# Cross-attention scores from float32r halves: four products stacked along the contraction, with loop orders and PSUM banks laid out anew

## The reference, cut to what matters

```
x  = layernorm(x + linear_attention(x))         # causal, relu features, out_w
q  = x; k = v = ctx                             # 16 heads of 8
scores = einsum('bhqd,bhkd->bhqk', qh, kh) / sqrt(8)
scores = where(|q - k| > 64, -inf, scores)
x  = layernorm(x + softmax(scores) @ v @ W_proj.T + b_proj)
x  = layernorm(x + switch_ffn(x))               # 8 experts, top 1, capacity 641, gelu, width 512
```

## Time and profile before

| | |
|---|---|
| time, median of 3 runs (lowest, highest) | 424.26 us (423.18, 426.59) |
| span of the profiled execution | 423.4 us |
| PE busy, share of the span | 393.0 us, 93% |
| DVE busy | 330.9 us, 78% |
| ACT busy | 269.4 us, 64% |
| POOL busy | 253.0 us, 60% |

### The profile page before, as it was taken

How to read it: one execution, slowest core, us unless ns; L and a number is a source line. 1 busy time by engine, 2 the same in 40 slices (tenths; PEclk the granted TensorE clock), 3 DMA queues, 4 the chain that set the end, 5 groups by cost and what they waited for, 6 DMA issues and landing times.

```text
span 423.4 us, 19225 instructions
## 1 busy us (share of the span) xinstructions
PE 393.0 (93%) x7095; PEld 297.0 (70%) x7095; DVE 330.9 (78%) x1640; ACT 269.4 (64%) x610; POOL 253.0 (60%) x372
## 2 busy tenths in 40 slices
PE   7889999999999999999999999999878999999960
PEld 6556777677777777677777777766566788888750
DVE  5465778889889888898989988878975588877760
ACT  4437777777877777777778776876646344444441
POOL 5243455676675776765775766576653077766653
PEclk8999999999999999999999999999999999999995
DMA  4900000101111011111102123000021334342000
GB/s 112 319 19 15 23 23 15 29 29 28 56 27 30 28 29 41 42 29 28 29 29 53 31 53 96 15 23 10 28 67 36 98 118 138 117 130 89 26 21 21
DMA packets 25859, 22.74 MB, mean 54 GB/s; under 512 B 3623, under 2 KB 21090, under 8 KB 25766
## 3 DMA queue, kind: packets, MB, share of 16 engines
q1 hardware_dynamic: 23430, 17.30, 14.0%
q0 software_dynamic: 2336, 4.20, 3.1%
HBM read 12.46 MB, written 9.58 MB: 52 GB/s over the span
## 4 chain that ended last, share of the span: by engine, by line
PE 74%; ACT 9%; issue 5%; POOL 4%; DVE 3%; DMA 3%; SPq 1%; POOLq 0%; DVEq 0%; ACTq 0%
PE banks L769 13%; PE banks L719 13%; PE banks L1200 8%; PE banks L711 8%; ACT arena L1481 7%; PE banks L731 7%; PE banks L704 6%; PE banks L781 3%; PE banks L848 2%; PE banks L1180 2%; PE banks L797 2%; PE banks L749 2%; PE banks L751 2%; PE banks L750 2%; POOL expert_in L501 1%
## 5 line engine op out<-in xcount | busy, mean ns | idle before, releaser
L1681 DVE TENSOR_REDUCE mx<-banks 128x8 f32<-128x1024 f32 x64 | 77.0, 1220 | 19.5 <-PE banks L719 19.5
L1228 ACT ACTIVATE arena<-banks 128x1024 f32<-128x1024 f32 x64 | 62.1, 1022 | 42.8 <-PE banks L719 42.8
L769 PEld LDWEIGHTS banks<-arena,V 128*32 128x32 f32 x2048 | 53.3, 109 | 30.0 <-ACT arena L1258 23.5
L769 PE MATMUL banks<-arena,V 128*32 128x128 f32 x2048 | 67.5, 275 | 0.6 <-ACT arena L1258 0.3
L1258 ACT ACTIVATE arena<-banks 128x1024 f32<-128x1024 f32 x64 | 62.1, 1022 | 5.8 <-PE banks L711 5.8
L1481 ACT ACTIVATE arena<-banks,b1T 128x321 f32<-128x321 f32 x64 | 33.8, 529 | 42.9 <-PE banks L1180 42.2
L637 POOL DMA_INDIRECT out_x<-ot,idx x40 | 40.3, 1008 | 23.4 <-DVE ot L2314 11.0
L468 POOL TENSOR_TENSOR rs<-ve,minus_half 128x1 f32<-128x1 f32 x32 | 18.2, 569 | 54.5 <-DVE ve L1649 54.5
L485 POOL TENSOR_TENSOR rs<-ve,minus_half 128x2 f32<-128x2 f32 x32 | 23.2, 726 | 38.7 <-DVE ve L1669 38.6
L501 POOL DMA_INDIRECT expert_in<-x,sidx x32 | 35.1, 1098 | 15.1 <-issue 5.3
L462 POOL TENSOR_TENSOR QE<-qT,head_mask 128x512 f32<-128x512 f32 x32 | 33.1, 1034 | 9.4 <-DVE qT L1592 9.3
(11 more groups left out here) (210 smaller groups left out, 974.7 us busy)
## 6 DMA issues: line engine op xcount, KB each, us to landing
w_sb<-in_L_ffn_W SPq DMA_DIRECT2D x16, 256.0 KB, 3.1
EB<-expert_in SPq DMA_DIRECT2D x9, 325.0 KB, 4.0
expert_in<-zeros SPq DMA_DIRECT2D x10, 266.5 KB, 3.3
X<-in_x SPq DMA_DIRECT2D x32, 64.0 KB, 2.0
C<-in_ctx SPq DMA_DIRECT2D x32, 64.0 KB, 2.7
out_x<-fb SPq DMA_DIRECT2D x32, 64.0 KB, 2.3
out_x<-ot,idx POOLq DMA_INDIRECT x40, 2.2
b2b<-in_L_ffn_b SPq DMA_DIRECT2D x1, 512.0 KB
```

The costliest lines, as they stand in the source:

```text
L769: mm = pe.matmul(bank(name)[VW * s:VW * (s + 1), half * P:(half + 1) * P], V[:, h, :], scored[:, h // NA, h % NA, :], start=q == 0, stop=q ...
L1228: nc.scalar.activation(A1[b % 2][:, 2 * half:2 * half + 2].rearrange("p j a t -> p j (a t)"), pair("s1", half), ACT.Relu).then_inc(s1_out[ ...
L1681: v.tensor_reduce(mx[b % 2][:, 8 * half:8 * half + 8].rearrange("p (j a) -> p j a", a=NA), pair("s2", half).rearrange("p j (a t) -> p j a ...
```

## The change

- Turned x1 and turned ctx are split in a float32r high part and a float32r remainder. ACT writes the high part twice in one instruction (`op_x1h`, `op_ch`), DVE the remainder twice (`op_x1l`, `op_cl`). `x1p` holds high, high, low, low; `cp` holds high, low, high, low.
- SP spreads each 32 partitions x 4 parts over 128 partitions, four DMAs for x1 (`op_repX`) and four for ctx (`op_repC`) per batch, 64 KB each, from SBUF to SBUF. A strip of 32 partitions then holds, for one head, 8 dimensions x 4 parts: the contraction sums the four products high x high, high x low, low x high, low x low.
- `op_s2` and `op_s2t` each do 16 float32r matmuls of 32 rows by 128 columns (`by_stack`). CE, its four masked ACT instructions and x1T's copy are gone. Heads are ordered otherwise, and proj_w is loaded in a permuted order to match (two DMAs of 64-byte pieces).
- `op_xTe` and `op_y1Te` move from DVE to ACT. `op_pv1` and `op_pv2` are cut in halves a and b, masks get steps of their own (`op_s1m`, `op_s2m`, `op_s2tm`), the subtraction of maxima too (`op_s2x`).
- JOBS gives other banks: s1, s2 and s2t all use banks 6 and 7. All written-out orders change. `clear_rows` is spread over loads 4 to 8, expert weights are loaded at batches 16 and 17, `early_rows` is issued after `fallback(B - 3)`.

```diff
-JOBS = [("y1T", 2, (0,)), ("lg", 8, (7,)), ("xT", 0, (6,)), ("o2", 6, (6,)), ("o1", 2, (1,)), ("t2", 4, (6,)),
-        ("qkv", 0, (3,)), ("mxT", 3, (2,)), ("cT", 2, (7,)), ("s2t", 3, (0, 1, 4, 5)), ("rk", 8, (7,)),
-        ("x1T", 2, (0,)), ("pv1", 1, (5,)), ("s2", 2, (2, 3, 6, 7)), ("y2T", 5, (0,)), ("t1", 1, (7,)),
-        ("x2T", 7, (5,)), ("pv2", 3, (4,)), ("s1", 0, (1, 2, 4, 5))]
+JOBS = [("xT", (3,)), ("qkv", (4,)), ("s1", (6, 7, 0, 1)), ("pv1", (2,)), ("t1", (5,)),
+        ("y1T", (5,)), ("o1", (5,)), ("x1T", (1,)), ("cT", (2,)), ("s2", (6, 7, 4, 5)),
+        ("mxT", (4,)), ("s2t", (6, 7, 2, 3)), ("pv2", (3,)), ("t2", (0,)), ("y2T", (2,)),
+        ("o2", (4,)), ("x2T", (0,)), ("lg", (5,)), ("rk", (1,))]
...
-        x1T = ring("x1T", 2, [P, P])
-        CE = ring("CE", 4, [P, NA, P])
+        x1p, cp = ring("x1p", 2, [P, 4, P], F32R), ring("cp", 2, [P, 4, P], F32R)
+        x1s = ring("x1s", XS, [P, NA, P], F32R)
+        cs = ring("cs", CS, [P, NA, P], F32R)
...
+            def spread(stack, sem_in, parts):
+
+                for g in range(NA):
+                    sp.dma_start(stack[:, g, :].bitcast(F32), parts[VW * g:VW * (g + 1)].bitcast(F32)).then_inc(sem_in, 16)
+
+            def op_repX(b):
+                sp.wait_ge(x1h_done, b + 1)
+                sp.wait_ge(x1l_done, b + 1)
+                wait(sp, s2_full, b - XS + 1)
+                wait(sp, s2t_full, b - XS + 1)
+                k = b % 2
+                spread(x1s[b % XS], x1s_in[b % XS], x1p[k])
...
-            sp.dma_start(w_rows[:, 4, :], proj_w).then_inc(weights_in, 16)
+            for half in range(2):
+                sp.dma_start(w_rows[:, 4, half * D // 2:(half + 1) * D // 2].rearrange("o (s u) -> o s u", u=SLOT),
+                             proj_w.rearrange("o (s u) -> o s u", u=VW)[:, :, half * SLOT:(half + 1) * SLOT]).then_inc(weights_in, 16)
...
+            fallback(B - 3)
+            early_rows()
+            fallback(B - 2)
+            fallback(B - 1)
...
+            def by_stack(name, weights, moved, last):
+
+                for a in range(NA):
+                    for j, used in enumerate(BANKS[name]):
+                        part = slice(VW * j, VW * (j + 1))
+                        mm = pe.matmul(banks[:, used, a * P:(a + 1) * P], weights[part, a, :], moved[part, a, :],
                                        start=False, stop=last and a == NA - 1, tile_position=(VW * j, 0))
                 return mm
...
             def op_s2(b):
-                window_masks("s2", b)
-                pe.wait_ge(x1T_done, b + 1)
-                pe.wait_ge(CE_ready, b + 1)
-                by_slot("s2", x1T[b % 2], CE[b % 4]).then_inc(s2_full, 1)
+                stacked(pe, x1s_in, b)
+                stacked(pe, cs_in, b)
+                by_stack("s2", x1s[b % XS], cs[b % CS], True).then_inc(s2_full, 1)
...
             def op_s2t(b):
-                window_masks("s2t", b)
-                by_head("s2t", lambda part, a: CE[b % 4][part, a, :], lambda part, a: x1T[b % 2][part, :])
+                stacked(pe, x1s_in, b)
+                stacked(pe, cs_in, b)
+                by_stack("s2t", cs[b % CS], x1s[b % XS], False)
...
-            def op_CE(b):
+            def op_ch(b):
                 act.wait_ge(cT_full, b + 1)
-                wait(act, s2t_full, b - 3)
-                for a in range(NA):
-                    last = nc.scalar.activation(CE[b % 4][:, a, :], bank("cT")[:, 0:P], ACT.Copy,
-                                                scale=head_mask[:, a:a + 1])
-                last.then_inc(CE_ready, 1)
+                unstacked(act, cs_in, 2, b)
+                nc.scalar.copy(cp[b % 2][:, 0:4:2, :], twice("cT")).then_inc(ch_done, 1)
...
+            def remainder(low, name, high, done):
+
+                v.tensor_tensor(low, twice(name), high.bitcast(F32), ALU.subtract).then_inc(done, 1)
+
+            def op_x1l(b):
+                dve.wait_ge(x1h_done, b + 1)
+                unstacked(dve, x1s_in, 2, b)
+                remainder(x1p[b % 2][:, 2:4, :], "x1T", x1p[b % 2][:, 0:2, :], x1l_done)
```

More of the change, by code:

```diff
@@ L377, in early_rows @@
                 sp.dma_start(ER0[:], buf[ET * P:ROWS, :]).then_inc(early_in, 16)
[L379 to L390 removed]
+            load(4)
```

2081 lines of the change are left out of this document (1350 added, 731 removed).

## The result

The changed kernel takes 464.35 us (median of 4 runs, 461.7 to 468.19), the kernel before 425.42 beside it (423.18 to 427.6): a ratio of 1.0952, with an interval of 1.0902 to 1.1003. It is slower by 39 us, where 413 was forecast. The profiled execution has a span of 466.4 us (before 423.4) and a mean granted TensorE clock of 0.935 of full speed (before 0.981); it is the slowest of the four (468.19 us).

A forecast was written before the change was run, and what follows sets the result against it. PE bounds the kernel now; DVE was to take over at 8.5 us a period instead of 8.99. Span 423.4 - 13.2 (27 periods) + 1.5 (start) + 0.5 (tail) = 412.2, median 0.9 above: 413 us, range 400 to 428.

The forecast's parts named there:

- I take 0.48: PE's score groups: 16 float32r matmuls would take 0.48 us, against 0.95 for op_s2t's float32 ones.
- rival 1: PE's score groups: float32r at 128 columns no faster than float32, giving 431 to 432 us; chance 0.12.
- 8.99 - 1.03 + 0.2 = 8.16: PE's need per period in us: old period, less score groups' saving, plus two more tiling changes from cutting pv2.
- DVE becomes the bound: Middle of the loop: DVE needs 8.5 us a period, more than PE's 8.16, so the period is 8.5.
- two circles: Dependency loops: through SP's spread DMAs, 7.6 to 8.3 us; over banks 6 and 7, 8.05; both under the period.
- Rival 3: DVE does not stall: dependent pairs cost nothing, DVE and PE need 8.1 us each, total 402 us; chance 0.18.
- mxh, r2 and mxs 0.45: DVE steps behind the two maxima, cast, op_res2 and subtraction: 0.45 us together in the circle through SP.
- It stays just under 8.5, so I cost it at nothing: Circle from op_s2 through maxima, SP's issues and DMA landing to the next op_s2: 7.6 to 8.3 us, hidden.
- rival 2: The way through DMA sets the period: 424 to 425 us at a 3.3 us landing, 443 at 4.0; chance 0.15.
- I take 0.5: Tail: early_rows also waiting for fallback(B - 3) costs 0.5 us, bounds 0 and 3.
- I take 1.5: Start: proj_w in 1024 pieces of 64 bytes and one more issue delay PE's weight turn by 1.5 us.
- I count 0 and bound it by 0 and 2: Start: the first op_s2's wait for four issues and a landing, 3.9 us more, costs 0 net.

The follow-up runs named there:

- Runs 1 and 6: 1: kernel before with only x1T and CE made float32r, 419.7 us; 6: changed kernel with float32 in place of float32r, 480.52 us.
- run 4: Changed kernel with one spread DMA of four and row maxima over half of the keys: 438.62 us, ratio 1.0339.
- Run 10: Changed kernel with one spread DMA of four and POOL's two bias additions moved ahead of op_pow1 in the loop: 441.39 us, ratio 1.0394.
- run 2: Changed kernel with one spread DMA of four for x1 and for ctx: 448.18 us, ratio 1.0523.
- run 14: Changed kernel with all four spread DMAs issued, each moving a quarter of the bytes: 459.0 us, ratio 1.0809.
- Run 12: Run 10's kernel with ACT's evictions of s1 and exponentials of s2t halved from batch 24 on: 440.69 us.
- run 8: Changed kernel with one spread DMA of four and the writes of out issued by ACT instead of SP: 450.3 us.
- run 9: Changed kernel, all four spread DMAs kept, with POOL's two bias additions moved ahead of op_pow1 in the loop: 463.7 us.
- Run 13: Run 10's kernel with DVE's cast of the maxima (op_mxh) written as a reduction over one element: 438.99 us.
- run 11: Changed kernel with one spread DMA of four and eight matmuls with zeros ahead of op_mxT in the last nine batches: 455.12 us.

## Why the prediction was wrong

**float32r: right.** "I take 0.48" for 16 matmuls; 0.51 was measured, one record each. Both score groups together save 0.97 us a period, where I had 1.03. Runs 1 and 6 show the gain: rival 1 (no faster) is out.

**PE's need: mis-sized.** "8.99 - 1.03 + 0.2 = 8.16"; run 4, where PE is full, has 8.77. That "there are two more changes of tiling a period" was a miscount. By the timelines PE changes between whole-array, row-tiled and column-tiled steps 5 times a period before and 11 times after, since the masks, the single turns and pv2a now stand between groups of another tiling. The values cost nothing more for being cut (0.70 and 1.45 us, before 2.18). All steps other than scores and values take 4.79 us of the period from 167.84 to 176.87 before and 5.51 of run 4's from 173.16 to 181.91, start to start: 0.72 for six changes, not 0.2 for two. Turns by themselves show it, before and after:

```profile
172.91 0.27 PE L704 MATMUL banks<-ident,y 128*128 128x128 f32 x1
173.02 0.28 PE L704 MATMUL banks<-ident,X 128*128 128x128 f32 x1
```

```profile
205.43 0.27 PE L859 MATMUL banks<-ident,C 128*128 128x128 f32 x1
...
207.37 1.52 PE L933 MATMUL banks<-arena,V 128*32 128x128 f32 x48
```

The turn of y before lets the next whole-array turn start 0.11 us later. After, column-tiled values follow the turn of C after 0.20 us (205.43 to 205.63) and the turn of y after 0.26 (207.11 to 207.37). That the changes of tiling are the cause of the whole 0.72 is argued from this count; no run takes them out one by one.

**"DVE becomes the bound": the step that failed.** DVE's sum of 8.31 was fair (26.9 to 27.4 busy of 30 at a period of 9.17 is 8.2 to 8.4, with the waits beside POOL in it). But a sum of work bounds a period from below only; PE's own sum is 8.77, above it, and the period was that of a circle over two engines, 9.17. I had summed two circles and left out this one: maxima, their turn, then everything that PE's written order puts between op_mxT and the next op_s2. In the kernel before, op_mxT stood a whole period behind its op_s2 and nothing waited for it; here it stands ten steps behind, and of DVE's 3.5 us PE's own steps cover only some 3. Against the forecast of 8.5 the middle period costs 0.27 us for PE's need and 0.40 for the circle, 15 us over the 23 periods from batch 1 to 24; the outliers cost 10 more. Rival 3, which had DVE without a stall, falls with it.

**One link grew: the cast.** "mxh, r2 and mxs 0.45"; measured from 209.62 to 210.48, 0.86, since cast and subtraction wait for POOL's additions. Run 10 gives this its weight: 0.36 us a period, nearly all that the circle has above PE's need (8.80 is left), and 6.8 us of time.

**"It stays just under 8.5, so I cost it at nothing": wrong by 16 us** (run 2). The circle through SP used 1.4 us for three issues ahead of the last; they take 1.9, and the group of four up to 3.3. With eight in a row and writes, loads and clearing in the same queue, what is held up once is handed on: op_s2t of batches 0 and 1 stand 14.78 us apart, before 8.97. Eleven of the 16 us hang on the number of issues (run 14). This was rival 2, with a chance of 0.15 and 443 us at its worst; it was right as to the place and wrong in that it does not set the middle period.

**The ends: "I take 0.5" for the tail; the late stretch and the way to the experts cost 25 us.** I had looked at `early_rows` alone, took the late orders as equal, and did not reckon with a lower granted clock. Shown: 4.9 us of the late stretch go with one DMA in place of four (run 2). Run 12 showed that ACT's evictions are not it, run 8 that SP's writes are not. The windows above put 16 of the 25 us down to PE's busy time at a lower granted clock, 6.3 of the 7.2 ahead of the experts among them. Other runs bear this out for that last stretch: with 176 or 177 records and 4.3 to 4.5 us of PE idle each, it takes 24.4 us in run 9 at a clock of 0.79, 27.1 in run 10 at 0.69 and 28.1 in run 2 at 0.63. Run 13, the best of the new layout, is even 4.2 us ahead of the kernel before at op_s2t of batch 24 (244.78 against 248.98) and loses all of its time behind it. What lowers the granted clock was not tested apart; PE has more idle time in the late stretch of every run of the new layout (from 6.3 us in run 11 to 11.5 in the changed kernel; 3.5 before), and PE's longer way from op_mxT to op_s2 is one source of it. How the rest divides stays open.

**The start: too dear in one place, too cheap in the other.** "I take 1.5": PE's weight turn behind `b_rows` starts at 8.01, before at 7.31, 0.7 later, and op_s2t of batch 0 at 31.73, 2.0 earlier than before. But "I count 0 and bound it by 0 and 2" for the four issues and the landing ahead of op_s2 fails: PE waits 4.2 us for x1s there, and op_s2t of batch 1 is 3.8 us late.

Taken together, by the times of runs 2, 10 and 13: 464.4 less 16.2 (DMAs), less 6.8 (POOL beside the cast, middle), less 2.4 (the reduction, not clear of noise) is 439.0, still 14 above the kernel before, with float32r's gain in it and three quarters of the spreads left out. As written, the layout does not pay; float32r in the old one does, by 1.6%.

## What to carry to other kernels

A period has another bound beside each engine's sum: for every value that crosses engines, add the in-order work of the engine that it comes back to, from the step that takes it to the step that sends the next one. A relayout by many small DMAs is priced by the issuing queue, count times 0.6 us here, before bytes and landing. Count every change of tiling in the new order, not only those of the step that is cut. Read the granted clock of each stretch before comparing lengths: new waits of PE in one place can go with dearer matmuls in the next. When a step moves, look at what the engine next to it does at that moment, GpSimd beside a small DVE copy above all.
